# A bound in place of the measured maximum of M, and a different route for Wv and two x tiles

## The chip, the core and the metric

The kernel runs on one core of one Trainium2 chip. The metric is the device time of one execution in microseconds, from launch to end. The core has five engines that run their own instruction streams and meet only at semaphores: PE (TensorE, matrix products), DVE (VectorE), ACT (ScalarE), POOL (GpSimd) and SP (SyncE, which here only issues DMAs).

## What is computed

`x` is 4096 x 512, `adj` is 4096 x 4096, all in float32. Layer 0 is an attention with the adjacency as an additive term, a residual and a layer norm; layer 1 is a two-step graph convolution with a residual and a layer norm:

```
q, k, v = x @ Wq.T + bq, x @ Wk.T + bk, x @ Wv.T + bv
a   = q @ k.T / sqrt(512) + adj + adj
x   = layernorm(x + softmax(a) @ v)
h   = relu(adj @ (x @ W1) + b1)
out = layernorm(x + adj @ (h @ W2) + b2)
```

## The kernel before

Every large product is done in float16 with each operand split into a high and a low half, three matmuls for one (high times high, high times low, low times high; lines 578 to 580). A split needs a scale, a power of two taken from a maximum over the whole operand. Such a maximum is taken on DVE or ACT along the rows, and over the 128 partitions by POOL's `partition_all_reduce`; then four linked DVE instructions on one column make the scale (`power`, lines 1152 and 1153, and `scale_of`, lines 1156 and 1157). In a linked instruction the next one waits for its end.

Queries and keys are folded: the logits are `x (Wq' Wk) x'` plus bias terms, so the kernel first makes M = Wq' Wk (512 x 512, float32 matmuls, line 601, into PSUM banks 0 to 3), and g = M' x' takes the place of the queries. The stages are:

1. Set-up, up to some 25 us. Weights and x arrive in eight groups of four tiles (`load_x`, line 356). PE makes M, two bias rows (`part_g`, line 607; `part_u`, line 610, which becomes `c_row`), and transposes Wv in 16 blocks (`wv_transposes`, line 590). ACT and DVE split the first four x tiles (`xt_hi`, `xt_lo`); SP transposes each split tile by DMA into xT (`transpose_x`, line 366). When M stands, DVE takes its maximum bank by bank (`m_max`, line 1149), POOL reduces it, and ACT and DVE split M (`m_hi`, line 866, `m_lo`).
2. The projection, from the first split of M to some 250 us. PE's order is fixed by hand: queries(0) to queries(3), values(0) to values(3), then for t = 4, 6, 8, ... queries(t), queries(t+1), values(t), values(t+1). A unit is 12 float16 matmuls of 512 columns. `queries(n)` needs for n = 4g all four tiles of x group g transposed into xT, and a free bank, which `g_hi(n-4)` gives. `values(t)` needs for t of 4 and more the bank that `v_full(t-4)` gives.
3. Attention, some 1300 us, and layer 1, some 400 us.

ACT's order around the change is: sum of half of x group 0, four `xt_hi`, sum of group 1, copy of the bias row, four `m_hi`, `g_hi(0)`, four `wv_hi`, `xt_hi(4)` to `xt_hi(7)`, `g_hi(1)` to `g_hi(3)`, sum of group 2, then in turn `v_hi(t)` and the sum of x group t + 3 for t = 0 to 4. From `t = 4` on, `xt_hi(8)` to `xt_hi(11)` stand ahead of `v_hi(4)`. DVE has the counterpart: in its loop over t stand `v_full(t)`, `query_bias(t+1)`, `v_lo(t)`; `g_scale(1)` stands behind `v_lo(2)`, `v_scale(1)` and `x_scale(2)` behind `v_lo(3)`, and then come `xt_lo(8)` to `xt_lo(11)`. `xt_hi(8)` waits for `x_scale(2)`.

SP's queue is, in order: Wq, Wk, x group 0, Wv, x group 1; transposes of x tiles 0 to 3; the row bv; x groups 2 and 3; transposes of tiles 4 to 7; x groups 4 to 7; transposes of tiles 8 to 11, and so on.

Of the kernel before, what the change touches and what calls it, by code (L numbers as in the profile page):

```python
# [15 lines left out]
P = 128  # L16
# [5 lines left out]
XS = 4  # L22
X_FIRST = 2
# [144 lines left out]
def gnn_program(nc, x, adj, wq, bq, wk, bk, wv, bv, w1, b1, w2, b2, out, x1_dram, g_dram, at_dram, y_dram):  # L168
    with ExitStack() as ctx:
# [6 lines left out]
        def flat(ap):  # L176
# [39 lines left out]
        names = ["m0", "m1", "m2", "m3", "st_wv", "st_w1", "mx_wv", "mx_w1", "e_wv", "e_w1", "s_wv", "s_w1",  # L216
                 "st_m", "st_gb", "mx_m", "mx_gb", "e_m", "s_m", "mx_bv", "c0p", "c0", "t0", "t1", "u0", "u1", "bound",
# [72 lines left out]
        m_bank = bank[0:4]  # L290

# [4 lines left out]
        wv_bank = bank[4:8]  # L296

        def queries_bank(n):
# [15 lines left out]
            sem(s) for s in ("d_small", "d_bv", "d_w1", "d_b1", "d_wv", "d_late"))  # L314
        d_w0, d_wr = sem("d_w0"), sem("d_wr")
# [14 lines left out]
        p_wv, p_pre, p_v, p_g, p_qk, p_pv, p_y, p_adj, p_x1, p_unit, p_h, p_o, p_end = (  # L330
            sem("p_" + s) for s in "wv pre v g qk pv y adj x1 unit h o end".split())
# [15 lines left out]
        def _(sp):  # L347
# [36 lines left out]

            for t in range(XS):
                transpose_x(t)
            sp.dma_start(bv_row, bv.rearrange("(o d) -> o d", o=1).broadcast_to([P, D])).then_inc(d_bv, 16)
            for i in range(X_FIRST, X_FIRST + 2):
                load_x(i)
            for t in range(XG, 2 * XG):  # L390
                transpose_x(t)
            for i in range(X_FIRST + 2, NT // XG):
                load_x(i)
            for t in range(NT):
                for q in x_tiles_at(t):
                    transpose_x(q)
# [179 lines left out]
        def _(pe):  # L576
# [11 lines left out]
            def wv_transposes(j):  # L588
                for k in range(KD):
                    last = pe.transpose(wv_bank[j][:, P * k:P * (k + 1)], wv_raw[:, k, P * j:P * (j + 1)], ident)  # L590
                last.then_inc(p_wv, 1)
# [13 lines left out]
            pe.wait_ge(v_part, 3)  # L605
# [4 lines left out]
            pe.matmul(bank[7][:, :], ones, part_u, start=True, stop=True).then_inc(p_pre, 1)  # L610
            pe.wait_ge(d_wv, 16)
            pe.wait_ge(g_id, 2)
            wv_transposes(0)
            wv_transposes(1)
            pe.wait_ge(v_gb, 2)
            wv_transposes(2)
            pe.wait_ge(a_bias, 1)
            wv_transposes(3)

            def values(t):  # L620
                if t >= V_BANKS:
                    pe.wait_ge(v_vf, t - V_BANKS + 1)
                if t % XG == 0:
                    for i in range(XS):
                        pe.wait_ge(d_xt[i], 16 * (t // XG + 1))
                for k in range(KD):
                    if t == 0:
                        pe.wait_ge(a_wv, k + 1)
                        pe.wait_ge(v_wv, k + 1)
# [25 lines left out]
            for t in range(XG):  # L655
                values(t)
# [188 lines left out]
        def _(act):  # L845
# [12 lines left out]
            def xt_hi(t):  # L858
                if t in BATCH_STARTS:
                    act.wait_ge(v_sx, batch(t) + 1)  # L860
                if t >= XS:
                    act.wait_ge(d_xt[t % XS], 16 * (t // XS))
                act.activation(x_split[t % XS][:, 0:D], xv[:, t, :], ACT.Identity, scale=col[f"s_x{batch(t)}"]).then_inc(a_xt, 1)

            def m_hi(k):
                act.activation(m_hl[:, 0, k, :], m_bank[k][:, :], ACT.Identity, scale=col["s_m"]).then_inc(a_m, 1)
# [22 lines left out]
            def wv_hi(k):  # L889
                act.wait_ge(p_wv, k + 1)  # L890
                act.activation(wvT[:, 0, k, :], wv_bank[k][:, :], ACT.Identity, scale=col["s_wv"]).then_inc(a_wv, 1)

            group_sum(0)
            for t in range(XS):
                xt_hi(t)
            group_sum(1)
            act.wait_ge(p_pre, KD + 3)
            act.activation(c_row, bank[7][:, :], ACT.Copy).then_inc(a_bias, 1)
# [24 lines left out]
            for i in range(XS):  # L923
                act.wait_ge(d_xt[i], 16 * len(range(i, NT, XS)))
# [53 lines left out]
            def x1_hi(r):  # L978
# [3 lines left out]
                else:  # L982
                    for i in range(XS):
                        act.wait_ge(d_xt[i], 16 * len(range(i, NT, XS)))
# [155 lines left out]
        def _(dve):  # L1140
# [10 lines left out]
            def power(dst, src):  # L1151
                link(dve.tensor_scalar(dst, src, TINY, None, ALU.max))
                link(dve.tensor_scalar(dst.bitcast(U32), dst.bitcast(U32), EXP_BITS, None, ALU.bitwise_and))

            def scale_of(dst, power_of):
                link(dve.reciprocal(dst, power_of))
                return dve.tensor_scalar(dst, dst, TOP, None, ALU.mult)
# [13 lines left out]
            def wv_max(i, rows):  # L1171
                link(abs_max(col[f"t{i}"], flat(wv_raw[:, rows, :])))

            def m_max(k):
                dve.wait_ge(p_pre, k + 1)
                link(abs_max(col[f"m{k}"], m_bank[k][:, :]))

            def wv_lo(k):
                dve.wait_ge(a_wv, k + 1)
                minus_hi(wvT[:, 1, k, :], wv_bank[k][:, :], col["s_wv"], wvT[:, 0, k, :]).then_inc(v_wv, 1)  # L1180
# [4 lines left out]

            def x_scale(b):
                dve.wait_ge(g_ar, (1, 2, 6, 7)[b])
# [5 lines left out]
            def v_scale(b):  # L1193
                link(dve.tensor_scalar(col[f"k_v{b}"], col[f"e_x{b}"], col["e_wv"], 1 / TOP ** 2, ALU.mult, ALU.mult))
                link(dve.tensor_scalar(col["bound"], col[f"k_v{b}"], 4.0 * TOP ** 2, col["mx_bv"], ALU.mult, ALU.add))
# [69 lines left out]
            dve.tensor_reduce(col["st_wv"], cols("t0", "t1"), AX, ALU.max).then_inc(v_st, 1)
# [380 lines left out]
```

## Time and profile before

| | us |
|---|---|
| median of 3 runs | 1907.13 (1907.11 to 1907.28) |
| the profiled execution | 1907.61 |
| its span, first to last instruction | 1905.8 |
| PE busy | 1897.2 (100%) |
| DVE busy | 1082.8 (57%) |
| ACT busy | 857.4 (45%) |
| POOL busy | 116.0 (6%) |

The profile is of one execution. Its span leaves out 1.8 us that lie around it. All times in the rows are counted from the start of the span. PE's granted clock reads full in all of its 40 slices. Matmuls overlap, so the start of one row tells more than its length.

### The profile page before, as it was taken

The numbers are of one execution on the slowest core, as the hardware profiler recorded it, in microseconds if no ns is written. First come the engines' busy times: TensorE is split into PE (matmuls) and PEld (weight loads), VectorE is DVE, ScalarE is ACT, GpSimd is POOL, SyncE is SP. The second block draws the span as 40 slices with busy tenths as digits, with TensorE's granted clock in tenths as the row PEclk, the third lists the DMA queues.
The fourth block names the chain that finished last, engine by engine and source line by source line (L and its number), as shares of the span: only waits on it lengthen the run. The fifth ranks groups of instructions, "written<-read, shape, count | busy, mean of one in ns | idle before, by whom it ended". The sixth has DMA issues, their size and how long they took to land.

```text
span 1905.8 us, 26547 instructions
## 1 busy us (share of the span) xinstructions
PE 1897.2 (100%) x9273; PEld 889.8 (47%) x9273; DVE 1082.8 (57%) x2107; ACT 857.4 (45%) x1838; POOL 116.0 (6%) x210
## 2 busy tenths in 40 slices
PE   9999999999999999999999999999999999999998
PEld 4444444444444444444444444444444454444446
DVE  7786666666666666666666666666666620001334
ACT  5654455555555455555555555555545611010112
POOL 0000000000000000000000000000000000002334
PEclk9999999999999999999999999999999999999999
DMA  7665599999999999999999999999999999989996
GB/s 234 164 138 123 127 231 227 225 231 227 227 223 226 228 229 228 227 224 226 225 230 225 229 226 231 226 222 226 228 222 237 215 349 387 387 307 358 395 394 244
DMA packets 798903, 463.21 MB, mean 243 GB/s; under 512 B 644656, under 2 KB 652592, under 8 KB 798768
## 3 DMA queue, kind: packets, MB, share of 16 engines
q1 hardware_dynamic: 790704, 447.51, 93.4%
q10 hardware_dynamic: 8064, 14.00, 2.0%
q8 instruction: 73, 1.20, 0.3%
q14 instruction: 62, 0.51, 0.1%
HBM read 220.99 MB, written 92.01 MB: 164 GB/s over the span
## 4 chain that ended last, share of the span: by engine, by line
PE 98%; DVE 1%; DMA 0%; issue 0%; POOL 0%; SPq 0%; ACT 0%; POOLq 0%; DVEq 0%; ACTq 0%
PE bank L578 15%; PE bank L580 15%; PE bank L579 15%; PE bank L690 12%; PE bank L691 12%; PE bank L692 12%; PE bank L814 5%; PE bank L813 5%; PE bank L815 5%; DMA adj_in<-in_L_gnn_Wk 0%; PE bank L777 0%; PE bank L774 0%; PE bank L773 0%; PE bank L834 0%; PE bank L835 0%; PE bank L836 0%
## 5 line engine op out<-in xcount | busy, mean ns | idle before, releaser
L959 ACT ACTIVATE tsp<-ring,sc 128x512 f16<-128x512 f32 x248 | 179.0, 722 | 599.3 <-DMA tsp<-tsp 598.5
L1341 DVE SCALAR_TENSOR_TENSOR ring<-bank,sc,adj_in 128x512 f32<-128x512 f32 x256 | 192.2, 751 | 396.1 <-PE bank L580 391.1
L578 PE MATMUL bank<-xT,gT 128*128 128x512 f16 x1024 | 388.1, 379 | 0.0
L579 PE MATMUL bank<-xT,gT 128*128 128x512 f16 x1024 | 388.1, 379 | 0.0
L580 PE MATMUL bank<-xT,gT 128*128 128x512 f16 x1024 | 388.1, 379 | 0.0
L690 PE MATMUL bank<-xv,tsp 128*128 128x512 f16 x1008 | 382.0, 379 | 0.0
L691 PE MATMUL bank<-xv,tsp 128*128 128x512 f16 x1008 | 382.0, 379 | 0.0
L692 PE MATMUL bank<-xv,tsp 128*128 128x512 f16 x1008 | 382.0, 379 | 0.0
L1160 DVE SCALAR_TENSOR_TENSOR tsp<-adj_in,s_a,tsp 128x512 f16<-128x512 f32 x248 | 184.7, 745 | 48.3 <-ACT tsp L967 47.9
L1160 DVE SCALAR_TENSOR_TENSOR tsp<-ring,sc,tsp 128x512 f16<-128x512 f32 x248 | 184.8, 745 | 0.1
L947 ACT ACTIVATE ring<-ring,bias 128x512 f32<-128x512 f32 x256 | 180.9, 707 | 7.4 <-DVE bias L1358 7.4
L1349 DVE TENSOR_REDUCE r_max<-ring 128x1 f32<-128x512 f32 x256 | 175.7, 686 | 8.8
L967 ACT ACTIVATE tsp<-adj_in,s_a 128x512 f16<-128x512 f32 x248 | 175.1, 706 | 3.9 <-DMA tsp<-tsp 3.6
L935 ACT ACTIVATE junk<-adj_in 128x512 fp8e4<-128x512 f32 x256 | 157.0, 613 | 10.1 <-DMA adj_in<-in_adj 10.0
L579 PEld LDWEIGHTS bank<-xT,gT 128*128 128x128 f16 x1024 | 100.2, 98 | 120.8
L578 PEld LDWEIGHTS bank<-xT,gT 128*128 128x128 f16 x1024 | 100.2, 98 | 120.8
L580 PEld LDWEIGHTS bank<-xT,gT 128*128 128x128 f16 x1024 | 100.2, 98 | 120.8
L692 PEld LDWEIGHTS bank<-xv,tsp 128*128 128x128 f16 x1008 | 98.6, 98 | 118.9
L690 PEld LDWEIGHTS bank<-xv,tsp 128*128 128x128 f16 x1008 | 98.6, 98 | 115.3 <-DMA tsp<-tsp 0.5
L691 PEld LDWEIGHTS bank<-xv,tsp 128*128 128x128 f16 x1008 | 98.6, 98 | 114.8
L1503 DVE TENSOR_TENSOR xv<-bank,xv 128x512 f16<-128x512 f32 x8 | 5.5, 691 | 153.2 <-ACT xv L1048 153.2
L1054 ACT ACTIVATE tsp<-tsp,shift,rstd 128x512 f32<-128x512 f32 x31 | 25.2, 813 | 122.5 <-POOL shift L1618 122.4
(261 smaller groups left out, 2167.3 us busy)
## 6 DMA issues: line engine op xcount, KB each, us to landing
adj_in<-in_adj SPq DMA_DIRECT2D x256, 256.0 KB, 3.2
at_dram<-tsp SPq DMA_DIRECT2D x248, 256.0 KB, 3.2
xv<-at_dram SPq DMA_DIRECT2D x54, 1024.0 KB, 14.5
adj_in<-at_dram SPq DMA_DIRECT2D x29, 1024.0 KB, 14.4
xT<-at_dram SPq DMA_DIRECT2D x20, 1024.0 KB, 13.7
xv<-in_x SPq DMA_DIRECT2D x8, 1024.0 KB, 9.9
g_dram<-tsp SPq DMA_DIRECT2D x32, 256.0 KB, 4.0
gT<-g_dram SPq DMA_DIRECT2D x32, 256.0 KB, 3.6
```

Of the source, the lines that this page charges most:

```text
L578: pe.matmul(dst, ah, bh, start=first, stop=False)
L579: pe.matmul(dst, ah, bl, start=False, stop=False)
L580: return pe.matmul(dst, al, bh, start=False, stop=last)
L690: pe.matmul(dst, ah, vh, start=(kb == 0 and j == 0), stop=False)
L691: pe.matmul(dst, ah, vl, start=False, stop=False)
L692: last = pe.matmul(dst, al, vh, start=False, stop=(kb == KB - 1 and j == TW - 1))
L947: act.activation(p, p, ACT.Exp, bias=bias[:, r % 2:r % 2 + 1], scale=2.0, accum_out=r_sum[:, r % 2, kb:kb + 1]).then_inc(a_exp, 1)
L959: act.activation(p_split(e)[:, 0:BANK], p, ACT.Copy, scale=col[f"p_up{batch(TW * kb)}"]).then_inc(a_p, 1)
L967: act.activation(asp[a % 2][:, 0:BANK], adj_in[:, a % AR, :], ACT.Copy, scale=s_a[:, r:r + 1]).then_inc(a_ah, 1)
L1160: return dve.scalar_tensor_tensor(dst, src, scale, hi, ALU.mult, ALU.subtract)
L1341: dve.scalar_tensor_tensor(t, s_bank[s % S_BANKS][:, :], col[f"k_l{batch(s // KB)}{batch(TW * (s % KB))}"], adj_in[:, s % AR, :], ALU.mult ...
L1349: dve.tensor_reduce(r_max[:, r % 2, kb:kb + 1], ring[:, s % RING, :], AX, ALU.max).then_inc(v_max, 1)
```

## The change

- M's scale no longer comes from M. DVE takes for each row of Wk the maximum (`abs_max(m0..m3)`, one linked reduce of 512 and one of 1536 elements), ACT sums for each row of Wq the absolute values (four `row_sum` with an accumulator), DVE multiplies the two and takes the maximum, and POOL reduces it. This bounds each element of M by 512 times the result; the top is `TOP_M` and the scale can be made while PE is still at M. The four `m_max` are gone. For the scale of g the kernel now takes the maximum of M's high half (`st_mh`, a reduce of 128 x 2048 float16) and for the values that of Wv (`st_w`, a reduce of 128 x 2048 float32); both go in one POOL call with `st_gb`, and `g_scale(0)` and `v_scale(0)` wait for it.
- Wv's scale comes from a sum of absolute values by ACT (128 x 2048, with an accumulator) in place of two DVE reduces. Wv is split untransposed (`wv_hi`, `wv_lo` read SBUF) and transposed by four DMA transposes, issued by SP behind the loads of x groups 2 and 3. The 16 PE transposes are gone. `values(0)` waits for all four.
- Of the first four x tiles, tiles 2 and 3 are transposed on PE (8 blocks, between the second and the third quarter of M), and ACT and DVE split them from PSUM straight into xT. Tiles 0 and 1 go by DMA as before.
- The matmul of the bias row (`part_u`) moves behind `values(0)`, and with it three DVE partials, the copy by ACT and `g_hi(0)`.
- ACT's new order: four row sums, sum of group 0, `xt_hi(0)`, `xt_hi(1)`, sum of Wv, `xt_hi_pe(2)`, `xt_hi_pe(3)`, four `m_hi`, four `wv_hi`, sum of group 1, `xt_hi(4)` to `xt_hi(7)`, bias row, `g_hi(0)` to `g_hi(3)`, sum of group 2.

```diff
+            def x_transposes_first():
+                pe.wait_ge(d_x[0], 16)
+                pe.wait_ge(g_id, 2)
+                for t in range(X_DMA, XG):
+                    for k in range(KD):
+                        last = pe.transpose(x_bank[t - X_DMA][:, P * k:P * (k + 1)], xv[:, t, P * k:P * (k + 1)], ident)
+                    last.then_inc(p_xt, 1)
...
+                if e == 2:
+                    x_transposes_first()
...
-            pe.matmul(bank[7][:, :], ones, part_u, start=True, stop=True).then_inc(p_pre, 1)
-            pe.wait_ge(d_wv, 16)
-            pe.wait_ge(g_id, 2)
-            wv_transposes(0)
-            wv_transposes(1)
-            pe.wait_ge(v_gb, 2)
-            wv_transposes(2)
-            pe.wait_ge(a_bias, 1)
-            wv_transposes(3)
+
+            def bias_row():
+                pe.wait_ge(v_part, 3)
+                pe.matmul(bank[7][:, :], ones, part_u, start=True, stop=True).then_inc(p_pre, 1)
...
+                if t == 0:
+                    pe.wait_ge(d_wvt, 16 * KD)
...
+            values(0)
+            bias_row()
+            for t in range(1, XG):
...
             for i in range(X_FIRST, X_FIRST + 2):
                 load_x(i)
+            for k in range(KD):
+                sp.wait_ge(a_wv, k + 1)
+                sp.wait_ge(v_wv, k + 1)
+                sp.dma_start_transpose(wvT.rearrange("p two k e -> p (two k) e")[:, :, P * k:P * (k + 1)],
+                                       wv_split[:, k, :, :].rearrange("p two d -> p (two d)")).then_inc(d_wvt, 16)
...
+            act.wait_ge(d_w0, 16 * 2)
+            row_sum(0)
+            act.wait_ge(d_wr, 16 * 2)
+            for e in range(1, KD):
+                row_sum(e)
...
+            act.activation(x_junk[:, 0:KD * D], flat(wv_raw), ACT.Abs, accum_out=col["t1"], saturate=False).then_inc(a_ws, 1)
+            for t in range(X_DMA, XG):
+                xt_hi_pe(t)
             act.wait_ge(v_sm, 1)
             for k in range(KD):
                 m_hi(k)
-            g_hi(0)
             act.wait_ge(v_sc, 1)
             for k in range(KD):
                 wv_hi(k)
+            act.wait_ge(a_ws, 1)
+            group_sum(1)
             for t in range(XG, 2 * XG):
                 xt_hi(t)
+            act.wait_ge(p_pre, KD + 3)
+            act.activation(c_row, bank[7][:, :], ACT.Copy).then_inc(a_bias, 1)
+            g_hi(0)
...
+            for k in range(1, KD):
+                m_lo(k)
+            dve.wait_ge(v_sc, 1)
             for k in range(KD):
-                m_max(k)
-            dve.tensor_reduce(col["st_m"], cols("m0", "m3"), AX, ALU.max).then_inc(v_st, 1)
+                wv_lo(k)
...
+            link(abs_max(col["st_gb"], gb_c[:, :]))
             x_scale(1)
             for t in range(XG, 2 * XG):
                 xt_lo(t)
+            for e in range(1, KD):
+                partial(part_u, wq_raw, bk_c, e)
+            link(abs_max(col["st_mh"], m_hl[:, 0, :, :].rearrange("p k e -> p (k e)")))
+            abs_max(col["st_w"], flat(wv_raw)).then_inc(v_st, 1)
             dve.wait_ge(d_bv, 16)
             link(abs_max(col["mx_bv"], bv_row))
+            dve.wait_ge(g_ar, 5)
+            link(dve.tensor_scalar(col["mx_mh"], col["mx_mh"], 2.002 * TOP, None, ALU.mult))
+            link(dve.tensor_scalar(col["mx_w"], col["mx_w"], 2.0, None, ALU.mult))
+            g_scale(0)
             v_scale(0)
+            g_lo(0)
+            g_lo(1)
```

## Rows read from the trace of the kernel before

**Rows 1.** Page, part 4: shares of the chain that ended last, by engine.

```profile
PE 98%; DVE 1%; DMA 0%; issue 0%; POOL 0%; SPq 0%; ACT 0%; POOLq 0%; DVEq 0%; ACTq 0%
```

**Rows 2.** Waits of PE, whole span: us in total, times, longest us.

```profile
PE bank L578 <- DVE ring L1160: 1.4, 1, 1.4
```

**Rows 3.** Timeline of PE, set-up: start us, us, engine, line [idle before, releaser].

```profile
0.97 4.21 PE L595 MATMUL bank<-tsp 128*128 128x128 f32 x18 [0.97 <-POOL tsp L1566]
5.29 14.83 PE L601 MATMUL bank<-adj_in 128*128 128x512 f32 x32
19.96 0.95 PE L607 MATMUL bank<-tsp 128*128 128x1 f32 x8
...
20.99 1.10 PE L610 MATMUL bank<-tsp 128*128 128x512 f32 x2
21.93 1.91 PE L590 MATMUL bank<-junk,adj_in 128*128 128x128 f32 x16
25.21 0.38 PE L578 MATMUL bank<-xT,ring 128*128 128x512 f16 x1 [1.36 <-DVE ring L1160]
```

**Rows 4.** Timeline of PE around the first matmul of queries(8).

```profile
66.68 0.38 PE L578 MATMUL bank<-xT,ring 128*128 128x512 f16 x1
```

**Rows 5.** Timeline of ACT, set-up.

```profile
12.27 1.06 ACT L855 ACTIVATE gT<-xv 128x1024 fp8e4<-128x1024 f32 x1 [9.34 <-DMA xv<-in_x]
...
15.79 1.33 ACT L863 ACTIVATE ring<-xv,sc 128x512 f16<-128x512 f32 x2 [2.37 <-DVE sc L1157]
...
23.49 2.42 ACT L866 ACTIVATE ring<-bank,sc 128x512 f16<-128x512 f32 x4 [0.76 <-DVE sc L1157]
```

**Rows 6.** Timeline of DVE, set-up.

```profile
12.69 1.22 DVE L1240 TENSOR_REDUCE x_sum<-xv 128x1 f32<-128x1024 f32 x1
...
19.20 2.86 DVE L1149 TENSOR_REDUCE sc<-bank 128x1 f32<-128x512 f32 x4
...
24.31 2.73 DVE L1160 SCALAR_TENSOR_TENSOR ring<-bank,sc,ring 128x512 f16<-128x512 f32 x4 [0.26 <-ACT ring L866]
...
28.54 1.75 DVE L1149 TENSOR_REDUCE sc<-adj_in 128x1 f32<-128x1536 f32 x1
```

**Rows 7.** Timeline of POOL, set-up.

```profile
22.34 0.35 POOL L1576 PARTITION_ALL_REDUCE sc<-sc  x1 [1.64 <-DVE sc L1248]
```

**Rows 8.** Timeline of ACT, g_hi(1), sums of groups 2 and 4, v_hi(2).

```profile
36.84 0.78 ACT L882 ACTIVATE adj_in<-bank,gb_s,sc 128x512 f32<-128x512 f32 x1
...
40.85 1.89 ACT L855 ACTIVATE gT<-xv 128x2048 fp8e4<-128x2048 f32 x1
...
47.81 1.91 ACT L855 ACTIVATE gT<-xv 128x2048 fp8e4<-128x2048 f32 x1 [1.66 <-DMA xv<-in_x]
...
49.72 0.70 ACT L873 ACTIVATE xv<-tsp,sc 128x512 f16<-128x512 f32 x1
```

**Rows 9.** Timeline of DVE, g_scale(1) and v_full(3) behind it.

```profile
51.13 0.21 DVE L1201 TENSOR_SCALAR sc<-sc 128x1 f32<-128x1 f32 x1
...
52.72 0.74 DVE L1216 SCALAR_TENSOR_TENSOR adj_in<-bank,sc,x1T 128x512 f32<-128x512 f32 x1
```

**Rows 10.** Timeline of SP: x groups 2 and 3, transposes of tiles 8, 9 and 11.

```profile
23.54 0.99 SPq L356 DMA_DIRECT2D xv<-in_x  x2
...
58.77 2.60 SPq L366 DMA_TRANSPOSE xT<-ring  x2
...
62.85 1.29 SPq L366 DMA_TRANSPOSE xT<-w_hl  x1
```

**Rows 11.** DMA issues, 0 to 60 us: median us to landing stands last.

```profile
xT<-ring SPq DMA_TRANSPOSE x5, 3.2
```

**Rows 12.** Windows: busy us of PE, PEld, DVE, ACT, POOL, PEclk, DMA share, GB/s.

```profile
25.00:26.00 1.00, 0.79 (x4) 0.35 (x5) 1.00 (x3) 0.91 (x2) 0.00 (x0) 1.00 0.39 96
...
28.00:29.00 1.00, 1.00 (x6) 0.48 (x5) 0.92 (x4) 0.28 (x1) 0.00 (x0) 1.00 1.03 403
...
32.00:33.00 1.00, 1.00 (x6) 0.42 (x5) 0.78 (x3) 0.91 (x2) 0.00 (x0) 1.00 0.35 121
```

More of the change, by code:

```diff
@@ L22 @@
 XS = 4
+X_DMA = 2
 X_FIRST = 2
@@ L328, in gnn_program @@
         d_out = [sem(f"d_out{i}") for i in range(O_RING)]
-        p_wv, p_pre, p_v, p_g, p_qk, p_pv, p_y, p_adj, p_x1, p_unit, p_h, p_o, p_end = (
-            sem("p_" + s) for s in "wv pre v g qk pv y adj x1 unit h o end".split())
+        p_xt, p_pre, p_v, p_g, p_qk, p_pv, p_y, p_adj, p_x1, p_unit, p_h, p_o, p_end = (
+            sem("p_" + s) for s in "xt pre v g qk pv y adj x1 unit h o end".split())
+        a_rs, a_ws = sem("a_rs"), sem("a_ws")
         a_w2, v_w2, v_z, v_o = sem("a_w2"), sem("v_w2"), sem("v_z"), sem("v_o")
@@ L383, in store_g @@
                                  ).then_inc(d_gout[g % 2], 16)
-            for t in range(XS):
+            for t in range(X_DMA):
                 transpose_x(t)
@@ L860, in xt_hi, with row_sum, xt_pe, xt_hi_pe @@
                     act.wait_ge(v_sx, batch(t) + 1)
-                if t >= XS:
-                    act.wait_ge(d_xt[t % XS], 16 * (t // XS))
+                if t >= XS and x_transposes(t - XS):
+                    act.wait_ge(d_xt[t % XS], 16 * x_transposes(t - XS))
                 act.activation(x_split[t % XS][:, 0:D], xv[:, t, :], ACT.Identity, scale=col[f"s_x{batch(t)}"]).then_inc(a_xt, 1)
+            def row_sum(e):
+                if e:
+                    act.wait_ge(a_rs, e)
+                act.activation(x_junk[:, 0:D], wq_raw[:, e, :], ACT.Abs, accum_out=row_sums[:, e:e + 1], saturate=False).then_inc(a_rs, 1)
+            def xt_pe(part, t):
+                return xT[:, 0, part, :, P * t:P * (t + 1)]
+            def xt_hi_pe(t):
+                act.wait_ge(p_xt, t - X_DMA + 1)
+                act.activation(xt_pe(0, t), x_bank[t - X_DMA][:, :].rearrange("p (k n) -> p k n", n=P), ACT.Identity,
+                               scale=col["s_x0"]).then_inc(a_xt, 1)
             def m_hi(k):
+                act.wait_ge(p_pre, k + 1)
                 act.activation(m_hl[:, 0, k, :], m_bank[k][:, :], ACT.Identity, scale=col["s_m"]).then_inc(a_m, 1)
@@ L889, in wv_hi @@
             def wv_hi(k):
-                act.wait_ge(p_wv, k + 1)
-                act.activation(wvT[:, 0, k, :], wv_bank[k][:, :], ACT.Identity, scale=col["s_wv"]).then_inc(a_wv, 1)
+                act.activation(wv_split[:, k, 0, :], wv_raw[:, k, :], ACT.Identity, scale=col["s_wv"]).then_inc(a_wv, 1)
+            act.wait_ge(d_w0, 16 * 2)
[3 more added lines that the diff above has]
+                row_sum(e)
+            act.wait_ge(a_rs, KD)
             group_sum(0)
-            for t in range(XS):
+            for t in range(X_DMA):
                 xt_hi(t)
-            group_sum(1)
-            act.wait_ge(p_pre, KD + 3)
-            act.activation(c_row, bank[7][:, :], ACT.Copy).then_inc(a_bias, 1)
+            act.wait_ge(d_wv, 16)
+            act.wait_ge(a_xs, 1)
+            act.activation(x_junk[:, 0:KD * D], flat(wv_raw), ACT.Abs, accum_out=col["t1"], saturate=False).then_inc(a_ws, 1)
+            for t in range(X_DMA, XG):
+                xt_hi_pe(t)
             act.wait_ge(v_sm, 1)
@@ L923, in _ @@
             for i in range(XS):
-                act.wait_ge(d_xt[i], 16 * len(range(i, NT, XS)))
+                act.wait_ge(d_xt[i], 16 * x_transposes(NT - XS + i))
             act.wait_ge(v_scales, 1)
@@ L1184, in xt_lo, with xt_lo_pe @@
                 minus_hi(x_split[t % XS][:, D:2 * D], xv[:, t, :], col[f"s_x{batch(t)}"], x_split[t % XS][:, 0:D]).then_inc(v_xt, 1)
+            def xt_lo_pe(t):
+                dve.wait_ge(a_xt, t + 1)
+                hi, lo = (xT[:, 0, part, :, P * t:P * (t + 1)] for part in range(2))
+                minus_hi(lo, x_bank[t - X_DMA][:, :].rearrange("p (k n) -> p k n", n=P), col["s_x0"], hi).then_inc(v_xt, 1)
             def x_scale(b):
-                dve.wait_ge(g_ar, (1, 2, 6, 7)[b])
+                dve.wait_ge(g_ar, (1, 4, 6, 7)[b])
                 link(dve.tensor_reduce(col["mx_x"], x_all[:, X_COLUMNS[b]], AX, ALU.max))
```

120 lines of the change are left out of this document (58 added, 62 removed).

## Prediction

> **What bounds the kernel now.** I read the chain that ended last first, then PE's waits, then PE's timeline. The chain is 98% PE [rows 1]. PE's waits over the whole span come to little, and the one that matters here is the 1.4 us before the first split of M is there [rows 2]. From 25.21 us on PE runs without a gap: 16 units lie between the first matmul of queries(0) at 25.21 and that of queries(8) at 66.68 [rows 3, 4], and 41.47 / 16 = 2.592 us a unit is 12 matmuls at 0.216. So in this kernel a change to the set-up is worth what it moves PE's stream, and from there every later microsecond stays where it is, unless PE meets a wait that it doesn't meet now. The question has two halves: how early can PE be, and do DVE, ACT and SP still deliver on time once they carry what PE and the early set-up gave up?
>
> **PE's own side.** M runs from 5.29 to 19.96, the two small products to 20.99, the bias row takes 0.94 to 21.93, the 16 transposes of Wv 1.91, and then PE is idle until 25.21 [rows 3]. A block is 1.91 / 16 = 0.12, so the 8 blocks of x cost 0.96 within M. x is there at 12.27 [rows 5], before the third quarter of M (19.96 less 16 passes of 0.43 is 13.1), so no wait is added. M ends at 20.9, the small products at 21.95. The scale of M: ACT's start of xt_hi(0) at 15.79 hung on DVE's sum of x at 12.69; with less DVE work ahead the sum starts at about 12.3, as x lands, and xt_hi(0) at 15.35. Behind it stand on ACT two tiles at 0.62 (1.33 for two, less one overlap) [rows 5], the sum of Wv at 1.91 [rows 8], and two tiles from PSUM at 0.58 (2.42 for four: (2.42 - 0.69) / 3) [rows 5]: m_hi(0) at 19.65. The bound's own way, a POOL call of 0.35 with some 0.1 on either side [rows 7] and four small instructions on DVE, is over by about 18.2 and is hidden. m_lo(0) starts at 20.5; but DVE makes Wv's scale between m_lo(0) and m_lo(1), so the four low halves end at 21.3, 22.6, 23.25 and 23.9 (0.66 apart, (2.73 - 0.75) / 3 [rows 6], and 0.64 for the scale). PE starts queries(0) at 21.95, is held up by some 0.2, 0 and 0 us at the next three, and ends queries(3) at about 32.5, where it now ends at 35.58. **PE is 3.1 us early there, and pays the bias row of 0.94 later: 2.2 us is the most that can be had.**
>
> **The Wv transposes.** wv_hi starts at 21.95, the four wv_lo end at 24.55, 25.2, 25.85 and 26.5, and SP issues a transpose every 1.36 us (62.85 - 58.77 over three) [rows 10], so the last is issued at 28.7. Alone it would land 3.2 us later [rows 11], at 31.9, in time for 32.5. But the queue is in order, as the loads of groups 2 and 3 show: issued from 23.54 on [rows 10], they move nothing at 25 to 26, where the row bv trickles at 96 GB/s, run at 403 GB/s at 28, and are done at about 32.35 [rows 12]. In the changed kernel the same loads are issued 3.3 us earlier (xt_lo(0) ends at 16.85, two transposes take 1.36 each to 19.65, bv's issue some 0.6: 20.25 for 23.54), so they are done at about 29.1. Four transposes of 1.35 us end at 34.5 and the last lands at about 35.1. **values(0) then starts at 35.1, not at 32.5: 2.6 of the 3.1 us are given back**, and behind the bias row PE stands 0.45 us later than now. The bounds are 31.9 and 35.1; I take the upper, because bv and the two loads behind it show the order kept. PE alone would reach queries(8) at 67.1 (or at 64.5, if the transposes pass the loads).
>
> **The chain on ACT and DVE.** This is the part that PE's early start says nothing about. What g_hi(0) needs has been moved behind much work. In the changed kernel:
> - four m_hi from 19.65 (2.3), four wv_hi from 21.95 (2.45), the sum of group 1 (2.0 with its accumulator) to 26.4; POOL 0.55; x_scale(1) five small instructions, 0.95; xt_hi(4) at 27.9. DVE is free at 26.9, so ACT sets this.
> - xt_lo(4) at 28.65, four at 0.66: 31.3. Three partials of part_u, the first two linked (0.75 + 0.03), 2.25: 33.55.
> - Reduces of 2048 elements. 512 take 0.69 and 1536 take 1.75 [rows 6], so 2048 take 2.28 in float32. Two, 4.5: 38.05. The one over M's high half reads float16, which no row shows; its bounds are 1.14 (half) and 2.28. I take 2.28, since the rows at hand are of the same instruction.
> - bv's maximum 0.71, POOL's answer at 38.9, two small ones 0.38: g_scale(0) at 39.3. It takes 1.59 (52.72 - 51.13) [rows 9] and the way to ACT 0.15: **g_hi(0) at 41.05**, and g_hi(1) at 42.4, where it now starts at 36.84 [rows 8].
> - g_hi(0) to g_hi(3) 5.35 ((40.85 - 36.84) / 3 = 1.34 each) [rows 8]: sum of group 2 at 46.4, where it now starts at 40.85.
> - From that sum to v_hi(2) it takes now 49.72 - 40.85 = 8.87, of which 1.66 is a wait for x group 4 [rows 8]. Those loads now land earlier, so 7.2: v_hi(2) at 53.6. DVE's v_full(0) to v_full(2) fit beside it.
> - From v_hi(2) to the transpose of tile 8 it takes 58.77 - 49.72 = 9.05, all of it DVE and ACT passing work to and fro (g_scale(1), v_full(3), v_hi(3), v_lo(3), v_scale(1), x_scale(2), xt_hi(8), xt_lo(8)): 62.65. The fourth transpose is issued 4.08 later and lands 3.2 after that [rows 8, 10, 11]: tile 11 at 69.95, PE 0.05 behind.
>
> Now the same sum gives 62.85 + 3.2 = 66.05 against PE's 66.68: there were 0.6 us to spare. **In the changed kernel queries(8) starts at 70.0 in place of 66.68, 3.3 us later**, whatever PE saved before: its own arrival at 67.1 or 64.5 only sets how long it waits, 2.9 or 5.5 us. Queries(4) (at 46.4 against g_hi(0)'s end at 41.8) and values(4) (at 51.6 against v_full(0) at 46.6) have room. Behind queries(8) the order is as now and shifted alike; SP is then 3.9 us late and PE 3.3, so the next group keeps over 1 us of room.
>
> The Trainium skill bears on one price. VectorE: DVE Perf Modes, section on the perf-mode tier table, says that tensor_reduce has only the 1x form, whatever the type, so the reduce over M's high half would get no faster for being float16. With the opposite the sum would be 1.1 us less; no row here shows it.
>
> **Sum.** The profiled time is 1907.61 with a span of 1905.8, and the median of the runs 1907.13. The change adds 3.3 to either: 1907.13 + 3.3 = **1910.4 us**, 0.17% slower. What a measurement of this kernel can tell from no change is about 0.2%, 3.8 us; the forecast lies inside it, near its end.
>
> **Rivals.**
> 1. *The chain keeps up.* If the reduces, the POOL call and the ACT pairs take less than I sum (3.3 us less), queries(8) isn't held and PE's own side decides: 1907.13 + 0.45 = 1907.6 with the Wv transposes behind the loads, 1907.13 - 2.2 = 1904.9 with them in time. For it: 0.6 us of room now, and the range of the float16 reduce gives 1.1. Against: the 5.6 us of delay at g_hi(1) shrink only to 3.9 at tile 8, and none of its terms is a guess but one. 0.13.
> 2. *PE's clock falls during the wait* (the slower side). The stream's first 18 passes of 128 columns take 4.21 us, 0.21 each, the Wv blocks of the same width 0.12 [rows 3]: after the idle start PE ran at the lower of its two levels, 1.2 in place of 2.4 GHz, and the idle 1.36 us at 25 did not bring that back. If the wait at queries(8) does, a stretch like the first, some 4 us, is run at half speed and costs 2 us more: 1912.4. It decides if the wait is long, 5.5 rather than 2.9 us, and so hangs on Wv's transposes being in time. TensorE: Matmul & The Clock Gate in the Trainium skill, part 1, says that an idle array goes back to the lower level; the 1.36 us here is no test of it. 0.17.
> 3. *The delay isn't absorbed once but twice*: queries(12) is late as well, its room of over 1 us gone because DVE and ACT, shifted against PE, wait for products in between. By what its room lacks, some 1 to 2 us: 1912. 0.10.
> 4. *The bound doesn't reach*: m_lo waits on something of the new way (row sums on ACT behind the weights) and PE starts late too. It changes PE's side alone and leaves the end at 1910.4; it is in the forecast's chance.
>
> **Chances.** Forecast 0.60, rivals 0.13, 0.17 and 0.10. The forecast's own spread is 1909.3 (float16 reduce at half) to 1911.3; perhaps a sixth of its chance lies over 1910.9. Slower by over 0.2%: 0.10 + 0.17 + 0.10 = 0.37. Faster by over 0.2% would need 3.8 us where 2.2 are to be had: 0.02. The rest, 0.61, is within. The range runs from 1906.8, inside rival 1, to 1912.7, which takes in rival 2.
>
> **What would show each step.** PE's first f16 matmul at 22.0, values(0) starting near 35.1 behind a wait for the transposes of Wv, the bias row behind it; g_hi(0) near 41; the sum of group 2 near 46.4; the transpose of tile 8 issued at 62.7; a PE wait of some 3 us at queries(8), starting at 70.0, and the rest of the stream 3.3 us late with no other wait; the granted clock full all through. It is wrong if that wait is missing or over 4 us, if a further one stands at queries(12), or if matmuls behind it are 0.43 apart.

## The result and the profile after

The changed kernel takes 1911.98 us (median of 9 runs, 1910.81 to 1914.19) and the kernel before 1907.28 us (9 runs, 1907.11 to 1908.02). The ratio is 1.0026, 95% interval 1.0016 to 1.0036: slower, by 4.7 us. The forecast was 1910.4, in a range of 1906.8 to 1912.7. The runs of the changed kernel also spread over 3.4 us, those of before over 0.9.

The profiled execution took 1911.98 us with a span of 1910.2, 4.4 us more than before. PE's waits over the whole span (engine, line waited for: us in total, times, longest us) now hold two that answer to the single one of [rows 2]:

```profile
PE bank L598 <- DMA ring<-xT: 3.3, 1, 3.3
...
PE bank L598 <- DMA xT<-w_hl: 1.0, 1, 1.0
```

L598 is the first of the three float16 matmuls of a term, L578 before. The first wait is for the DMA transposes of Wv, ahead of values(0); the second is for the transpose of tile 11, ahead of queries(8). The timeline of PE shows both, and between them something that neither explains:

```profile
12.82 1.04 PE L613 MATMUL bank<-junk,xv 128*128 128x128 f32 x8
13.70 7.03 PE L626 MATMUL bank<-adj_in 128*128 128x512 f32 x16
20.57 0.95 PE L632 MATMUL bank<-tsp 128*128 128x1 f32 x8
...
21.79 0.38 PE L598 MATMUL bank<-xT,ring 128*128 128x512 f16 x1
...
35.77 0.39 PE L598 MATMUL bank<-ring,xT 128*128 128x512 f16 x1 [3.29 <-DMA ring<-xT]
36.00 0.38 PE L599 MATMUL bank<-ring,xT 128*128 128x512 f16 x1
...
38.34 0.63 PE L598 MATMUL bank<-ring,xT 128*128 128x512 f16 x1
38.77 0.63 PE L599 MATMUL bank<-ring,xT 128*128 128x512 f16 x1
...
39.62 1.46 PE L638 MATMUL bank<-tsp 128*128 128x512 f32 x2
40.92 0.38 PE L598 MATMUL bank<-ring,xT 128*128 128x512 f16 x1
...
70.53 0.38 PE L598 MATMUL bank<-xT,ring 128*128 128x512 f16 x1 [0.95 <-DMA xT<-w_hl]
```

Queries(0) starts at 21.79 where it started at 25.21 [rows 3]: PE's own side of the change works as meant. Behind queries(3) it is idle for 3.29 us, and 1.3 us into values(0) the matmuls are 0.43 apart instead of 0.216. The bias row (L638) falls into that stretch. Queries(8) starts at 70.53, 3.85 us later than in [rows 4]. The windows show the clock (busy us of PE, PEld, DVE, ACT, POOL, PEclk, DMA share, GB/s):

```profile
34.00:36.00 2.00, 0.23 (x2) 0.11 (x2) 1.97 (x2) 0.00 (x0) 0.00 (x0) 1.00 1.16 233
36.00:38.00 2.00, 2.00 (x9) 0.85 (x8) 2.00 (x2) 0.00 (x0) 0.00 (x0) 0.77 0.96 185
38.00:40.00 2.00, 2.00 (x6) 1.02 (x5) 1.77 (x8) 0.00 (x0) 0.38 (x1) 0.50 1.03 196
40.00:42.00 2.00, 2.00 (x7) 0.60 (x6) 1.71 (x10) 0.88 (x2) 0.00 (x0) 0.88 0.80 107
```

The granted clock goes to 0.50, the lower of the two levels (1.2 GHz), at about 37 and is back at about 40.5. In all of the profile of the kernel before it reads full.

The other engines, DVE first (the two reduces of 2048 elements, g_scale(0) at L1253), then ACT (bias row copied, g_hi(0), sum of group 2, v_hi(2), xt_hi(8)), then SP (the Wv transposes, those of tiles 8 and 11):

```profile
33.48 2.28 DVE L1203 TENSOR_REDUCE sc<-ring 128x1 f32<-128x2048 f16 x1
35.79 2.29 DVE L1203 TENSOR_REDUCE sc<-adj_in 128x1 f32<-128x2048 f32 x1
...
39.08 0.21 DVE L1253 TENSOR_SCALAR sc<-sc 128x1 f32<-128x1 f32 x1
```

```profile
41.12 0.60 ACT L960 ACTIVATE xr<-bank 128x512 f32<-128x512 f32 x1 [10.80 <-PE bank L638]
41.62 0.77 ACT L925 ACTIVATE adj_in<-bank,gb_s,sc 128x512 f32<-128x512 f32 x1
...
46.94 1.89 ACT L884 ACTIVATE gT<-xv 128x2048 fp8e4<-128x2048 f32 x1
...
53.85 0.71 ACT L916 ACTIVATE xv<-tsp,sc 128x512 f16<-128x512 f32 x1
...
61.37 1.33 ACT L892 ACTIVATE ring<-xv,sc 128x512 f16<-128x512 f32 x2 [1.07 <-DVE sc L1211]
```

```profile
24.49 9.20 SPq L406 DMA_TRANSPOSE ring<-xT  x4
...
63.02 2.62 SPq L379 DMA_TRANSPOSE xT<-ring  x2
...
67.11 1.28 SPq L379 DMA_TRANSPOSE xT<-w_hl  x1
```

The reduce over float16 takes as long as that over float32, 2.28 us. ACT is idle for 10.80 us until the bias row is there, and g_hi(0) follows it at 41.62, though DVE's g_scale(0), begun at 39.08, was done by 40.8. Tile 8 is transposed at 63.02 where it was at 58.77 [rows 10].

Of the 4.4 us, 3.85 are there at queries(8). The first product of softmax and values starts 3.8 us later than before (228.66 for 224.86) and the last 4.4 (1545.3 for 1540.9), so the other 0.5 is added during the attention. A wait of 0.2 us for a DMA is to be seen there; the rest I didn't trace.

### The profile page after: what moved, and what is told of

It is laid out like the page before. It is cut to its first block, busy times and chain, and to the rows that moved or that the text cites. A ratio compares the mean times of both kernels' runs of the same rounds, so it can differ in the third digit from the quotient of the medians.

```text
span 1910.2 us, 26545 instructions
## 1 busy us (share of the span) xinstructions
PE 1898.4 (99%) x9265; PEld 889.2 (47%) x9265; DVE 1085.3 (57%) x2107; ACT 861.7 (45%) x1848; POOL 116.0 (6%) x210
## 4 chain that ended last, share of the span: by engine, by line
PE 95%; DMA 1%; DVE 1%; ACT 1%; SPq 1%; issue 1%; POOL 0%; POOLq 0%; ACTq 0%; DVEq 0%
PE bank L598 14%; PE bank L600 14%; PE bank L599 14%; PE bank L719 11%; PE bank L720 11%; PE bank L721 11%; PE bank L842 5%; PE bank L844 5%; PE bank L843 5%; DMA xv<-in_x 0%; SPq L406 0%; PE bank L806 0%; PE bank L802 0%; PE bank L803 0%; PE bank L863 0%
## 5 line engine op out<-in xcount | busy, mean ns | idle before, releaser
L598 PE MATMUL bank<-xT,gT 128*128 128x512 f16 x1024 | 388.1, 379 | 0.0
L598 PEld LDWEIGHTS bank<-xT,gT 128*128 128x128 f16 x1024 | 100.2, 98 | 120.8
```

The source lines that it names most:

```text
L598: pe.matmul(dst, ah, bh, start=first, stop=False)
```

## The experiments

The theory (theory 1 in the expectations) was that of the forecast: **PE's stream is held at queries(8) by a chain on ACT and DVE that starts at g_hi(0)**; the fallen clock was taken to act through the late bias row. The rival (theory 2) was that the wait and the fallen clock at values(0) cost PE their own length. Every time below is a median beside the kernel before of the same call (1907.26 to 1907.34), and the queries(8) start is that of the profiled execution.

**The bias row ahead of values(0).**

```diff
-            values(0)
-            bias_row()
+            bias_row()
+            values(0)
```

> The changed kernel with the matmul of the bias row ahead of values(0) instead of behind it. In the changed kernel PE waits 3.29 us for the Wv transposes before values(0) (to 35.77), then its clock falls from 36.9 to 40.9, the bias row ends at 41.0 and g_hi(0) starts at 41.62; queries(8) starts at 70.53 against 66.68 before. Theory 1 (the chain on ACT and DVE that starts at g_hi(0) sets queries(8); the fallen clock only acts through the bias row): the bias row runs at 33.6 to 34.6 inside the wait, splits it into two short ones, the clock stays up, g_hi(0) starts at 40.9 where DVE's g_scale(0) lets it, queries(8) at 69.8, and the time is some 0.7 us under the changed kernel's 1912.0 with less spread (1911.2 or less). Theory 2 (what PE loses at values(0) is what costs): PE gains 0.94 + some 2 us of clock, so 1909.

Measured: 1911.31 us (1910.95 to 1912.55), ratio 1.0022 (1.0013 to 1.0031). PE's timeline and ACT's g_hi(0):

```profile
33.57 1.12 PE L638 MATMUL bank<-tsp 128*128 128x512 f32 x2 [1.14 <-DVE tsp L1223]
35.70 0.61 PE L598 MATMUL bank<-ring,xT 128*128 128x512 f16 x1 [1.00 <-DMA ring<-xT]
69.97 0.38 PE L598 MATMUL bank<-xT,ring 128*128 128x512 f16 x1 [1.52 <-DMA xT<-w_hl]
```

```profile
40.88 0.78 ACT L925 ACTIVATE adj_in<-bank,gb_s,sc 128x512 f32<-128x512 f32 x1 [5.55 <-DVE gb_s L1258]
```

g_hi(0) now waits for DVE and starts at 40.88, as expected, and queries(8) at 69.97 (69.8 expected). PE by itself would have been there 1.1 us earlier than in the changed kernel (68.45 for 69.58, the start less the wait), and of that 0.6 arrived: the chain, not PE, sets the time. The expectation that the clock stays up failed. Two waits of 1.14 and 1.00 us with the bias row between them brought it down just as well, and the same stretch at half speed stands behind them; it was hidden in the wait at queries(8).

**PE kept busy through the wait.** 15 float32 matmuls of ones before values(0).

```diff
+            for i in range(15):
+                pe.matmul(bank[7][:, 0:P], ones, ones, start=True, stop=True)
             values(0)
```

> The changed kernel with 15 more 128-column float32 matmuls of ones (some 3.2 us at full clock, results unused) on PE between queries(3) and values(0), where it otherwise waits 3.29 us. Nothing else moves. Theory 1 (chain on ACT and DVE): the clock stays at 2.4 GHz, the bias row ends near 39.4, g_hi(0) starts at 40.9 in place of 41.62, queries(8) at 69.8 in place of 70.53: 0.7 us less than the changed kernel, and its spread of 3.4 us over 9 runs shrinks to under 1 us. Theory 2 (clock fall costs PE's own time one for one): 2 us less. If the spread stays, it doesn't come from the clock.

Measured: 1911.06 us (1910.64 to 1912.80), ratio 1.0021 (1.0012 to 1.0030). In the profile the clock stays full there, g_hi(0) starts at 40.77 and queries(8) at 69.73. That is theory 1 to 0.1 us, and far from the 2 us of theory 2. The spread is 2.2 us and not under 1. Without the two slowest of the 11 runs it is 1.0 us, and those two read a mean clock of 0.998, the other nine 0.999 or 1.000. So the clock fell for longer in those two; where, no profile shows.

**The two long reduces cut to a quarter, alone and with the bias row moved.**

```diff
-            link(abs_max(col["st_mh"], m_hl[:, 0, :, :].rearrange("p k e -> p (k e)")))
-            abs_max(col["st_w"], flat(wv_raw)).then_inc(v_st, 1)
+            link(abs_max(col["st_mh"], m_hl[:, 0, 0, :]))
+            abs_max(col["st_w"], wv_raw[:, 0, :]).then_inc(v_st, 1)
```

> The changed kernel with the two maxima behind g_scale(0) and v_scale(0) taken over 512 of the 2048 elements of each partition (M's high half, Wv); three quarters of both maxima are left out. DVE's way to g_scale(0) is 3.2 us shorter (39.1 to 35.9). If DVE alone set g_hi(0), queries(8) would start 3.2 us earlier and PE's own arrival (69.4) would decide: 1.1 us less than the changed kernel. Theory 1 with the bias row as second gate: ACT's copy of the bias row still starts at 41.1, g_hi(0) at 41.6, queries(8) at 70.5: no change (within 0.3 us of the changed kernel).

> The same two short maxima together with the bias row ahead of values(0). Both gates of g_hi(0) are now early: g_scale(0) at 35.9, the bias row at 34.6, so g_hi(0) at 37.6. Theory 1: the transposes of tiles 8 to 11 are ready for queries(8) at 66.6, PE reaches it by itself at 66.9 (values(0) at 35.8, no fallen clock), so queries(8) starts at 66.9 with no wait: 0.2 us over the kernel before, 1907.5. Theory 2 (it is PE's time at values(0)): the same as the bias row ahead of values(0) alone.

Measured: alone 1911.82 us (1909.84 to 1913.27), ratio 1.0022 (1.0013 to 1.0031); with the bias row moved 1909.91 us (1907.70 to 1910.87), ratio 1.0012 (1.0003 to 1.0021). DVE and ACT of the first:

```profile
35.67 0.21 DVE L1253 TENSOR_SCALAR sc<-sc 128x1 f32<-128x1 f32 x1
```

```profile
41.05 0.60 ACT L960 ACTIVATE xr<-bank 128x512 f32<-128x512 f32 x1 [10.94 <-PE bank L638]
41.55 0.77 ACT L925 ACTIVATE adj_in<-bank,gb_s,sc 128x512 f32<-128x512 f32 x1
```

g_scale(0) is 3.4 us earlier and g_hi(0) doesn't move, because the bias row gates it: queries(8) at 70.64, no change. **Two gates stand in front of g_hi(0), and cutting one brings nothing.** With both cut, tile 8 is transposed at 59.10 and PE has no wait at queries(8) at all, as expected. But the time was expected at 1907.5 and came out 2.4 higher: values(0) started at 35.56, the clock fell, and as there was no wait left to hide it in, queries(8) started at 68.34. The three quickest of the 11 runs, 1907.70, 1908.08 and 1908.13, are near the expected time.

```profile
36.00:38.00 2.00, 2.00 (x6) 0.69 (x5) 1.72 (x10) 0.31 (x1) 0.00 (x0) 0.50 0.97 187
38.00:40.00 2.00, 2.00 (x8) 0.82 (x7) 1.33 (x6) 1.94 (x4) 0.00 (x0) 0.74 1.05 196
```

**The row bv behind the Wv transposes.**

```diff
-            sp.dma_start(bv_row, bv.rearrange("(o d) -> o d", o=1).broadcast_to([P, D])).then_inc(d_bv, 16)
             for i in range(X_FIRST, X_FIRST + 2):
                 load_x(i)
             for k in range(KD):
...
                                       wv_split[:, k, :, :].rearrange("p two d -> p (two d)")).then_inc(d_wvt, 16)
+            sp.dma_start(bv_row, bv.rearrange("(o d) -> o d", o=1).broadcast_to([P, D])).then_inc(d_bv, 16)
```

> The changed kernel with the DMA of the row bv issued behind the four transposes of Wv in place of ahead of the loads of x groups 2 and 3. If the queue is in order and the slow row (some 3 us at about 100 GB/s) is what holds the loads and so the transposes, these land at about 32.5 in place of 35.6 and PE's wait of 3.29 us before values(0) is nearly gone; if the transposes are held for another reason (SP's issue, the splits), it stays. Theory 1 (the chain on ACT and DVE sets queries(8)): the bias row ends at 36, g_hi(0) starts at 40.9, tile 11 lands at 69.8, and PE, there at 64.6, waits some 5 us for it: 0.7 us less than the changed kernel at best, and up to 2 us more than that if its clock falls in the long wait (1910.3 to 1912.3). Theory 2 (PE's wait at values(0) is the cost): 3 us less than the changed kernel, 1909.

Measured: 1913.98 us (1913.65 to 1914.32), ratio 1.0034 (1.0022 to 1.0047). It removed most of the first wait and made the kernel slower by 2 us; 1910.3 to 1912.3 had been expected, and 1909 by the rival. PE's timeline and windows:

```profile
33.47 0.39 PE L598 MATMUL bank<-ring,xT 128*128 128x512 f16 x1 [1.24 <-DMA ring<-xT]
69.57 0.58 PE L598 MATMUL bank<-xT,ring 128*128 128x512 f16 x1 [3.99 <-DMA xT<-w_hl]
```

```profile
66.00:68.00 2.00, 0.00 (x0) 0.00 (x0) 1.82 (x5) 0.94 (x2) 0.00 (x0) 0.99 0.99 194
68.00:70.00 2.00, 0.43 (x2) 0.19 (x3) 1.84 (x4) 2.00 (x3) 0.23 (x1) 0.50 0.80 188
70.00:72.00 2.00, 2.00 (x6) 0.69 (x5) 1.10 (x2) 1.97 (x4) 0.14 (x1) 0.50 0.84 214
72.00:74.00 2.00, 2.00 (x6) 0.73 (x5) 1.36 (x3) 0.91 (x2) 0.00 (x0) 0.50 1.21 299
74.00:76.00 2.00, 2.00 (x8) 0.78 (x7) 1.81 (x5) 0.72 (x1) 0.00 (x0) 0.80 1.16 262
```

Three things follow. The queue is in order: values(0) is 2.3 us earlier because a slow row of 256 KB no longer stands ahead of the loads. The chain keeps its date whatever PE does: queries(8) at 69.57 (69.8 expected). And PE's gain turned into a wait of 3.99 us, in which the clock fell; it stayed at half for some 5.2 us of work (69.57 to 74.8), and half of that, 2.6 us, is lost for good, since nothing behind queries(8) hides it. Another 0.5 us is waited for a DMA in the attention. In all five runs the mean clock reads 0.997.

**ACT's sums moved off the chain.** The sums of groups 2 and 3 go ahead of the copy of the bias row, and the condition for the others becomes:

```diff
-                if X_FIRST + 1 + t < NT // XG:
-                    group_sum(X_FIRST + 1 + t)
+                if X_FIRST + 2 <= t < NT // XG:
+                    group_sum(t)
```

> The changed kernel with ACT's sums of x groups 2 and 3 put into its idle time before the bias row (30.3 to 41.1), and those of groups 4 to 7 behind v_hi(4) to v_hi(7) instead of between v_hi(0) and v_hi(3). Same work, other places. Theory 1: the chain between g_hi(0) and tile 8 is shorter by what the sums held up, then bound by DVE; v_hi(2) starts 1.0 to 1.4 us earlier, queries(8) at about 69.4, where PE's own arrival is: 1 us less than the changed kernel. If ACT's sums are beside the chain: no change.

Measured: 1911.90 us (1910.60 to 1914.05), ratio 1.0024 (1.0015 to 1.0032). The chain did get shorter: from g_hi(0) (42.21) to the transpose of tile 8 (61.72) it is 19.5 us against 21.4 in the changed kernel (41.62 to 63.02). But in this execution the wait at values(0) was 4.35 us, the clock fell behind it, and PE reached queries(8) at 70.0 by itself, with tile 11 there before it. So it confirms the length of the chain, and the expected 1 us wasn't seen.

What was won at tile 8 is lost again by tile 12. ACT's timeline in this version (v_hi(4), v_hi(5), the sum behind it, g_hi(6)), then the same of the changed kernel, which has no sum there, and PE in this version at queries(12):

```profile
66.70 0.72 ACT L916 ACTIVATE xv<-tsp,sc 128x512 f16<-128x512 f32 x1 [1.42 <-DVE tsp L1269]
...
69.22 0.71 ACT L916 ACTIVATE xv<-adj_in,sc 128x512 f16<-128x512 f32 x1
69.83 1.90 ACT L884 ACTIVATE gT<-xv 128x2048 fp8e4<-128x2048 f32 x1
...
71.73 0.76 ACT L925 ACTIVATE adj_in<-bank,gb_s,sc 128x512 f32<-128x512 f32 x1
```

```profile
68.01 0.72 ACT L916 ACTIVATE xv<-tsp,sc 128x512 f16<-128x512 f32 x1 [1.42 <-DVE tsp L1268]
...
70.53 0.71 ACT L916 ACTIVATE xv<-adj_in,sc 128x512 f16<-128x512 f32 x1
71.14 0.76 ACT L925 ACTIVATE adj_in<-bank,gb_s,sc 128x512 f32<-128x512 f32 x1
```

```profile
91.51 0.38 PE L598 MATMUL bank<-xT,ring 128*128 128x512 f16 x1 [0.62 <-DMA xT<-w_hl]
```

The sum behind v_hi(5) now stands ahead of g_hi(6) and costs its 1.9 us, and DVE waits another 0.63 us for xt_hi(12), which stands behind the last sum. From v_hi(4) to the transpose of tile 12 it is 17.2 us (66.70 to 83.91) against 14.7 in the changed kernel (68.01 to 82.72). PE waits 0.62 us for tile 15, and queries(12) starts at 91.51, in the changed kernel at 91.31.

**All four first x tiles by DMA** (`X_DMA = 4`), one part of the change undone.

> One part of the change undone: all four first x tiles go by DMA, none is transposed on PE. PE's M is 0.96 us shorter, but the fourth tile lands at about 24, so queries(0) starts at 24.2 in place of 21.8; bv, the loads and the Wv transposes are 2.7 us later (values(0) at 38.4 in place of 35.8), the clock falls, the bias row ends at 44 and g_hi(0) starts at 44.5. Theory 1: queries(8) follows g_hi(0) by 28.9 us: 73.4, 2.9 us more than the changed kernel, 1914.5. If the end hung on DVE's g_scale(0) alone (39.1), nothing would change.

Measured: 1913.93 us (1913.21 to 1916.00), ratio 1.0036 (1.0023 to 1.0050). 1914.5 was expected. Queries(0) at 24.46 (24.2 expected), values(0) at 38.25 (38.4), g_hi(0) at 42.40 and queries(8) at 71.39. The last two are 2 us earlier than expected because PE waited only 1.72 us at values(0) and the clock stayed up, so the bias row was not held up. The clock fell at queries(0) instead, behind a wait of 3.25 us. Undoing this part costs 2 us, so the transposes on PE pay. Of the 2 us, 0.86 are there at queries(8) and 0.5 are a wait for a DMA in the attention; the other parts of the change weren't undone singly.

**The kernel before with one more reduce** between v_lo(2) and g_scale(1).

```diff
+                if t == 2:
+                    link(abs_max(col["t1"], flat(xv[:, XG:2 * XG, :])))
                 if t + 2 in BATCH_STARTS[1:]:
                     g_scale(batch(t + 2))
```

> The kernel before with one more linked reduce of 128 x 2048 float32 (2.28 us, result unused) on DVE between v_lo(2) and g_scale(1). It tests the room of 0.6 us at queries(8) in the kernel before. Theory 1: the transposes of tiles 8 to 11 are 2.3 us later, queries(8) starts 1.7 us later with a wait of 1.7 us and everything behind it too: 1908.9. If DVE has more slack than that, no change: 1907.3.

Measured: 1908.87 us (1908.70 to 1909.88), ratio 1.0009 (1.0000 to 1.0017). PE's timeline has the wait where none was:

```profile
67.85 0.38 PE L578 MATMUL bank<-xT,ring 128*128 128x512 f16 x1 [1.48 <-DMA xT<-w_hl]
```

2.28 us of work that no result uses cost 1.5 us, so the kernel before had about 0.7 us of room at queries(8), where 0.6 were reckoned. This is the plainest proof that the cover there was thin before the change. (In its profile queries(8) is only 1.17 us later than in [rows 4], but there the set-up ran earlier too: queries(0) starts at 24.74 where it is 25.21 in [rows 3].)

**Three versions that keep the change and shorten the chain.** All have the sums moved as above and POOL's call split, so that g_scale(0) waits for the reduce over M only and the one over Wv follows it. The first two have bv behind the Wv transposes; the second and third make x_scale(2) behind v_lo(1) already; the third has bv as in the changed kernel and the bias row ahead of values(0).

> A version that keeps the change and shortens the chain. On top of the changed kernel: bv's DMA behind the Wv transposes; the sums of x groups 2 and 3 in ACT's idle time before the bias row and those of groups 4 to 7 behind v_hi(4) to v_hi(7); and the POOL call for M's and g's maxima split from that for Wv's, so that g_scale(0) waits for one reduce of 2048 elements and not two, the one over Wv following it. Theory 1 (PE waits only if the ACT and DVE chain is later than PE): g_hi(0) at 38.4 (g_scale(0), bias row copied by 37.7), v_full(0) at 44.6, v_hi(2) at 50.2, tile 8's transpose at 59.4, tile 11 landed at 66.7; PE, there at 65.6, waits 1 us: queries(8) at 66.7 where the kernel before has 66.68: 1907.3, and up to 2 us more if the clock falls in the 1.2 us wait at values(0). If the sums and the reduce are beside the chain: 1910 or more.

> The version before this one in the list, and x_scale(2) on DVE moved from ahead of xt_lo(8) to behind v_lo(1), so that xt_hi(8) needn't wait for it at the end of the chain. Theory 1: tile 8's transpose some 0.9 us earlier (58.5), tile 11 at 65.8, PE's own arrival at 65.6: queries(8) at 65.8, 0.9 us less than the kernel before: 1906.4 where the clock stays up, up to 2 us more in executions where it falls at values(0).

> As the one before, but bv stays ahead of the loads and instead the bias row goes ahead of values(0), into PE's wait of 3.3 us. values(0) at 35.7 as with the bias row moved alone; PE reaches queries(8) at 66.8, chain ready at 65.8: no wait there, 1907.4; where the clock falls at values(0) (as it did in that kernel's profile) PE pays it in full, 1.7 us more: 1909.

Measured: 1909.99 us (1909.61 to 1910.27), ratio 1.0013 (1.0005 to 1.0022); 1907.66 us (1906.94 to 1909.51), ratio 1.0002 (0.9993 to 1.0011); 1909.60 us (1907.83 to 1911.77), ratio 1.0012 (1.0003 to 1.0021). The first, PE's timeline:

```profile
66.54 0.38 PE L598 MATMUL bank<-xT,ring 128*128 128x512 f16 x1 [0.86 <-DMA xT<-w_hl]
88.78 0.38 PE L598 MATMUL bank<-xT,ring 128*128 128x512 f16 x1 [1.36 <-DMA xT<-w_hl]
```

Queries(8) starts at 66.54 (66.7 expected), earlier than before, and then **queries(12) waits**. It is the moved sums again: from v_hi(4) (64.05) to the transpose of tile 12 (81.25) it is 17.2 us, as with the sums moved alone. I had reckoned up to queries(8) only, and missed 1907.3 by 2.7 us. The second has no wait at queries(8) in its profile, 0.3 us at queries(12), and a fallen clock behind a wait of 2.06 us at values(0); that profile is of the slowest of its 11 runs (1909.51). The version missed the 1906.4 expected where the clock stays up, and is as fast as the kernel before, no faster. The third pays its fallen clock in full (queries(8) at 68.72), as foreseen for that case. No version beat the kernel before.

## Why the prediction was right

**PE's own side** held. Queries(0) was put at 21.95 and started at 21.79, the 8 blocks lengthened M by 0.88 (12.82 to 13.70; 0.96 reckoned), and values(0) was put at 35.1 and started at 35.77. The step behind it, that the transposes run behind bv and the loads of groups 2 and 3 in an ordered queue, is shown by the version with bv behind them. The start of values(0) was put 0.7 us too early; the four were issued over 9.20 us and not at 1.36 each, and why they were slower than those of x wasn't tried.

**The chain** held nearly step by step: both reduces at 2.28 us, g_scale(0) at 39.08 (39.3), sum of group 2 at 46.94 (46.4), v_hi(2) at 53.85 (53.6), tile 8 at 63.02 (62.65), queries(8) at 70.53 (70.0). That it, and not PE's time, sets the end is shown by how constant its length is. From g_hi(0) to queries(8) it is 28.91 us in the changed kernel, 29.09 with the bias row moved, 28.96 with PE kept busy, 29.09 with the short reduces alone, 28.90 with bv behind and 28.99 with all tiles by DMA, while PE's wait at queries(8) was anything from 0.95 to 3.99 us. The sum had 28.95 (41.05 to 70.0). That wait was 0.95 us in the changed kernel where some 3 were forecast: PE was there by itself at 69.6 and not at 67.1, 0.7 us of it from the later values(0) and 1.6 from the clock.

**The term that was mis-sized** is g_hi(0), at 41.62 instead of 41.05. The forecast took DVE's g_scale(0) as its only gate and the bias row as done by then. The bias row runs behind values(0), in the stretch at half clock, and came at 41.0. With that stretch filled, g_hi(0) was at 40.77 and queries(8) at 69.73: 3.05 us over before, against the 3.3 forecast. So for queries(8) the middle of the forecast is right without the clock, and the clock through the bias row is 0.8 us of the profiled 3.85. The time is not: the median of that version is 3.8 us over the kernel before.

**Rival 2, the clock**, was real but at the wrong place. It was put behind the long wait at queries(8) and given 0.17; it happened behind the 3.29 us at values(0), for which the text had a wait of 2.6 us and didn't ask for the clock. There, 3.4 us at half speed were mostly hidden, since PE had another wait ahead. Where it came at queries(8), as in the version with bv behind, it cost 2.6 us against the 2 reckoned. The TensorE: Matmul & The Clock Gate page of the Trainium skill says in part 1 that an idle array goes back to the lower level, and the traces agree: the clock reads 0.50 behind the waits of 3.29 and 3.99 us.

**What is luck.** The sum named 3.3 us and 4.7 were measured. The range reached up to 1912.7 for the sake of a clock that falls at queries(8), and no clock fell there. What made 4.7 of it is something else: 3.05 us at queries(8) with the clock up, 0.8 of the clock through the bias row, some 0.5 added in the attention, and 0.3 by which the profiled execution of the kernel before lies over its median. 1911.98 is over the 1911.3 at which the forecast's own spread ended; that it still lies inside the range is in part luck.

**The spread** of 3.4 us stays in part open. The mean clock of the runs with the short reduces goes with their time: the five at or under 1910.63 read 0.999, and of the six at 1911.82 and above all but one read 0.998 or less. So do the two slowest with PE kept busy. In the changed kernel it doesn't (0.998 at 1910.81 and at 1914.19). A profile exists for one execution of each, so where the clock fell in the longer ones isn't shown.

Rival 1 (the chain keeps up) fell with the wait at queries(8), and rival 4 (PE starts late too) with queries(0) at 21.79. Rival 3 (queries(12) late as well) didn't come in the changed kernel, where queries(12) is 3.9 us late as queries(8) is, but did with the sums moved and in the first of the three versions. It was nearer than the "over 1 us of room" reckoned: tile 15 is issued at 87.88 where it was at 82.43, 5.45 us later and not 3.9, partly because the transposes of tiles 12 and 13 took 3.69 us of the queue where they took 2.60. That is 3.4 us ahead of queries(12), and such a transpose lands 3.1 to 3.3 us after its issue. The forecast of "within 0.2%" at 0.61 against "slower" at 0.37 came out on the other side of a boundary of 3.8 us: 4.7.

## What to carry to other kernels

When one engine never waits, ask of each edit what it makes late on the others, and reckon their chain up to every later point at which the busy engine needs it: here 3.4 us of earlier start were worth nothing against a chain with 0.7 us of room. Look for all gates of a step before one is cut, for the second holds the first's gain. And a wait on TensorE is not over when it ends: price the clock behind it, and whether a later wait hides that.

## What the runs showed of the hardware

- A single wait of 3.29 us on PE brought the clock from 2.4 to 1.2 GHz for 3.4 us of the following matmuls, and so did two waits of 1.14 and 1.00 us with the bias row between. Waits of 1.36 us [rows 3], 1.72 (all tiles by DMA), 1.27 and 1.24 (both with bv behind the transposes) did not; one of 2.06 did, and two of 1.14 and 1.33 with the bias row between. The one of 3.99 us was followed by some 5.2 us of work at the lower level.
- The first 18 float32 passes of 128 columns take 4.21 us, 0.23 each and not the 0.21 of the forecast [rows 3]; 30 passes of the same matmul, put before values(0) to keep PE busy, took 3.51, 0.12 each. So PE's first passes ran at the lower level, as the forecast read it, though the granted clock reads 1.00 in those first windows too.
- A maximum over 2048 elements takes 2.28 us on DVE from float16 and 2.29 from float32. VectorE: DVE Perf Modes in the Trainium skill (section on the perf-mode tier table) says that tensor_reduce has only the 1x form, and the trace agrees.
- Four DMA transposes of Wv's split into the ring were issued over 9.0 to 10.2 us with two 1 MB loads and a row of 256 KB ahead of them, 7.15 to 8.02 without the row ahead, and landed 5.3 us after their issue in the changed kernel; those of x take 1.36 each and land after 3.2. In the kernel with all tiles by DMA it was 11.94.
